# An expert's gate and up matmuls woven together, two in a row over the same tokens

## The chip, the cores and the metric

The kernel runs on one core of a Trainium2 chip. The metric is the device time of one execution in microseconds; before the change the median of three runs is 642.3 us (642.14 to 643.11).

## What is computed

4096 tokens of width 256 go through a cross-attention block and then through a mixture of 16 routed experts and one shared one. Everything is float32.

```
x = x + xattn(layernorm(x), ctx, ctx, mask)          # keys: 154 per batch
xf = layernorm(x)
logits = l2norm(xf) @ l2norm(gate_w).T               # 16 experts
scores = sigmoid(logits); top 8, weights normed to sum 1 -> combine
g = einsum('nd,edh->neh', xf, w_gate)                # D = 256, H = 128
u = einsum('nd,edh->neh', xf, w_up)
y = einsum('neh,ehd->ned', silu(g) * u, w_down)
out = x + einsum('ned,ne->nd', y, combine) + shared expert (same form, weight 1)
```

## The kernel before, in words

The tokens are cut into 8 chunks of 512. For each chunk the kernel runs 17 experts (expert 0 is the shared one), and beside the experts of chunk c it runs the attention, the second layernorm and the router of chunk c+1, in pieces that tables at the top of the file place at steps of the expert loop ("5.5" is behind the gate and up of step 5). No scheduler is at work: every engine has its own program, written out by hand, and executes it in order; semaphores join them.

Numbers stay float32 on the way, but the matmuls of the experts are made in three passes. Each operand is split into a high part (rounded to the fast float32 format of TensorE) and a low part (the rest), and `three_pass` (lines 394 to 400) issues high x high, high x low and low x high: lines 397, 398 and 399. So gate and up are each 2 (halves of D) x 3 = 6 matmuls of 512 columns, with weights as the stationary and tokens as the moving operand; `down` (L622) is 4 (tiles of tokens) x 3 = 12 matmuls of 256 columns. Gate, up and y have two PSUM banks each; expert e uses bank e mod 2 of gate and of up.

The chain of one expert e through the engines:

- PE: gate, 6 matmuls, then up, 6 matmuls (`gate`, `up`, both by `first_of`)
- ACT: `tanh_gate` (L880), reads the gate's bank
- DVE: `silu_up`: L1158 (silu, reads the gate's bank again) and L1162 (product with up's bank)
- POOL: `weighted` (L1358), times the tokens' routing weights
- ACT: `hidden_hi` (L887), and DVE: `hidden_lo` (L1168), the split of the result
- PE: `down`, 12 matmuls

What sets the order is the same loop on each engine, over steps s:

- PE: down(s), pieces of the front at s, gate(s+3) and up(s+3), pieces at s+.5
- ACT: tanh_gate(s+2), pieces at s, hidden_hi(s+1), in the first chunk the high part of a weight (L809), pieces at s+.5
- DVE: silu_up(s+2), pieces at s, hidden_lo(s+1), in the first chunk the low part of a weight (L1017), pieces at s+.5
- POOL: weighted(s+1), then its pieces

Waits that matter here: gate(e) waits until silu of e-2 has read its bank (`silu_done`), up(e) until the product of e-2 has read its bank (`prod_done`); down(e) waits for `h_hi` and `h_lo` of e, the two halves of the split.

Pieces of the front that are named below. On PE: `attend` at 5.5 and 6, which waits for the low part of the probabilities (`write_probs_lo`, DVE L1094 and L1096, themselves behind ACT L842 and L844 `write_probs_hi`); `logits` at 12 (L582, L584), which waits for the low part of the tokens (`write_t2_lo`, DVE L1068 twice, behind a DMA that brings the turned tokens back); `turn_z` (L589) and `turn_c` (L593), two small transposes of the router. On DVE: `swap_x2` (L1056) at 8.5, which starts that DMA's way, `ln2_scale` (L1032), `top_eight` and `weights` of the router. On POOL: `ln2_std` and `inverse_norm` (L1309 to L1341) and `add_bias` (L1320).

In the prologue of the first chunk the router's `turn_z(0)` stands between gate(0, 0) and up(0, 0):

```python
            gate(0, 0)
            turn_z(0)
            up(0, 0)
```

Of the kernel before, what the change touches and what calls it, by code (L numbers as in the profile page):

```python
# [17 lines left out]
HI, LO = 0, 1  # L18
# [17 lines left out]
def xattn_moe_kernel(nc, x, ctx, mask, Wq, bq, Wk, bk, Wv, bv, gate_w, w_gate, w_up, w_down,  # L36
                     sw_gate, sw_up, sw_down, out):
    B, S, D = x.shape
    KEYS = ctx.shape[1]
    E, _, H = w_gate.shape  # L40
    TOK = 512
    TILES = TOK // P
    HALF = TOK // 2
    CHUNKS = B * S // TOK
    KD = D // P
    NE = E + 1
# [7 lines left out]
    UP0, DN0 = KD * H, 2 * KD * H  # L54
    SCALE = float(D) ** -0.5
    REST = (B - 1) * KEYS
    AHEAD = 3
# [12 lines left out]
    with ExitStack() as stack:  # L70
        def sb(name, shape, dt=F32):
            return stack.enter_context(nc.sbuf_tensor(name, shape, dt))
# [5 lines left out]
        W = sb("W", [P, NE, 2, WCOLS], F32R)  # L78
# [4 lines left out]
        xT = sb("xT", [P, 2, 2, KD, TOK], F32R)  # L83
# [71 lines left out]
        def banks(name):  # L155
            return stack.enter_context(nc.psum_tensor(name, [P, 2, 512], F32))

        gate_ps, up_ps, y_ps, f_ps = (banks(n) for n in ("gate_ps", "up_ps", "y_ps", "f_ps"))
# [34 lines left out]
        FREE = 2  # L193
# [5 lines left out]
        def upto(c, per, k):  # L199

            return c * per + k
# [5 lines left out]
        def slot(c, e):  # L207

            return (NE * c + e) % 2

        def nxt(c, e):

            return (c, e) if e < NE else (c + 1, e - NE)

        def low_split(e):

            if e in POOL_SPLITS:
                return w_lo_pool, POOL_SPLITS.index(e) + 1
            return w_lo_dve, len([i for i in range(e + 1) if i not in POOL_SPLITS])
# [170 lines left out]
        def _(pe):  # L390
            mm = nc.tensor.matmul
            turn = nc.tensor.transpose

            def three_pass(ps, pairs, first, last):

                for i, ((lh, ll), (rh, rl)) in enumerate(pairs):
                    mm(ps, lh, rh, start=first and i == 0, stop=False)  # L397
                    mm(ps, lh, rl, start=False, stop=False)  # L398
                    ins = mm(ps, ll, rh, start=False, stop=last and i == len(pairs) - 1)  # L399
                return ins  # L400
# [186 lines left out]
            def turn_z(c):  # L587
                pe.wait_ge(z_read, upto(c, 1, 1))
                turn(f_ps[:, 0, 0:TILES * 2 * E], zT[:, 0:P], ident[:]).then_inc(z_turned, 1)  # L589

            def turn_c(c):
                pe.wait_ge(combined, upto(c, 1, 1))
                turn(f_ps[0:TILES * E, 1, 0:P], cw.rearrange("p j e -> p (j e)"), ident[:]).then_inc(c_turned, 1)  # L593

            def first_of(c, e, ps, col, free, done):
                i, par = slot(c, e), c % 2
                if e == 0:
                    pe.wait_ge(t2_hi, upto(c, 2, 2))
                    pe.wait_ge(t2_lo, upto(c, 2, 2))
                if c == 0:  # L600
                    pe.wait_ge(w_hi, e + 1)
                    pe.wait_ge(*low_split(e))
                    if e == 0:
                        pe.wait_ge(gate_split, 2)
                    if e == 1:
                        pe.wait_ge(a_read, 2)
                pe.wait_ge(free, upto(c, NE, e - 1 + FREE))
                ins = three_pass(ps[:, i, :], [((W[:, e, HI, col + k * H:col + (k + 1) * H],
                                                 W[:, e, LO, col + k * H:col + (k + 1) * H]),
                                                (xT[:, par, HI, k, :], xT[:, par, LO, k, :])) for k in range(KD)],  # L610
                                 first=True, last=True)
                ins.then_inc(done, 1)

            def gate(c, e):
                c, e = nxt(c, e)
                first_of(c, e, gate_ps, 0, silu_done, gate_done)

            def up(c, e):
                c, e = nxt(c, e)
                first_of(c, e, up_ps, UP0, prod_done, up_done)  # L620

            def down(c, e):  # L622
                i = slot(c, e)
# [57 lines left out]
            turn_ln2_first(1)  # L681
            keys_by_wq_rest(1)
            logits(0)
            gate(0, 0)
            turn_z(0)
            up(0, 0)
            gate(0, 1)
            up(0, 1)
            turn_c(0)
            values(2, f_ps[:, 0, 0:D])  # L690
            gate(0, 2)
            up(0, 2)
            values(3, f_ps[:, 1, 0:D])
            for c in range(CHUNKS):
                ahead = c + 1 < CHUNKS
                for s in range(NE):
                    if not ahead and s + AHEAD == NE - 1:

                        gate(c, NE - 1)
                        up(c, NE - 1)  # L700
                    down(c, s)
                    if ahead:
                        front(s, c + 1)
                    if (s + AHEAD < NE - 1 or ahead) and not (c == 0 and s == 1):
                        gate(c, s + AHEAD)
                        up(c, s + AHEAD)
                    if c == 0 and s == 0:

                        gate(c, s + AHEAD + 1)
                        up(c, s + AHEAD + 1)  # L710
                    if ahead:
                        front(s + .5, c + 1)

# [714 lines left out]
```

## Time and profile before

| what | value |
|---|---|
| median of 3 runs | 642.3 us |
| the profiled execution: its time | 641.74 us |
| its span, first to last instruction | 639.6 us |
| PE busy | 632.1 us (99%), 3690 matmuls |
| PE weight loads | 550.9 us (86%) |
| DVE busy | 464.7 us (73%) |
| POOL busy | 275.4 us (43%) |
| ACT busy | 234.6 us (37%) |
| DMA, share of 16 engines | 36% |
| granted clock of TensorE, mean | 0.999 |
| chain that ended last: PE's share | 92% |

A busy time is the union of an engine's instructions, and a matmul's record reaches to its modelled end, past the start of the next one: what a matmul costs in a dense stream is the distance from its start to the next start, not its length. What lies between the span and the execution's own time (2.1 us) is taken as fixed. A name such as "gate_ps<-xT,W" says what an instruction writes and what it reads.

### The profile page before, as it was taken

How to read it: one execution, taken by the hardware profiler on the slowest of the kernel's cores; microseconds unless marked ns; L12 is line 12 of the kernel's file. 1: busy time of each engine (PE TensorE's matmuls, PEld its weight loads, DVE VectorE, ACT ScalarE, POOL GpSimd, SP SyncE). 2: the span in 40 equal slices, each digit the busy share in tenths (PEclk: the TensorE clock that was granted, in tenths of full speed). 3: DMA queues.
4: the chain of work that ended last, by engine and by line, in shares of the span. 5: the costliest groups of instructions: out<-in, count | busy, mean ns of one | idle time of the engine just before them, and what ended most of it. 6: DMA issues, size and time to landing. Idle time of an engine off the chain costs nothing.

```text
span 639.6 us, 10415 instructions
## 1 busy us (share of the span) xinstructions
PE 632.1 (99%) x3690; PEld 550.9 (86%) x3690; DVE 464.7 (73%) x925; ACT 234.6 (37%) x500; POOL 275.4 (43%) x261
## 2 busy tenths in 40 slices
PE   8999999999999999999999999999999999999997
PEld 7688888988889888888888888888888888888886
DVE  3789887759876698767977689766987669575444
ACT  4745544332343324333242333324233332432221
POOL 2527576325533356233653346423562335423342
PEclk9999999999999999999999999999999999999999
DMA  7457562532315324333335232253151431242100
GB/s 206 100 178 218 162 169 44 201 101 73 83 35 182 109 67 99 111 107 119 68 68 188 70 117 66 34 200 108 67 98 38 162 109 46 53 133 101 66 2 33
DMA packets 112512, 67.04 MB, mean 105 GB/s; under 512 B 80981, under 2 KB 102254, under 8 KB 112462
## 3 DMA queue, kind: packets, MB, share of 16 engines
q1 hardware_dynamic: 111374, 65.61, 35.4%
q10 hardware_dynamic: 1088, 0.79, 0.4%
q8 instruction: 29, 0.48, 0.3%
q14 instruction: 21, 0.17, 0.1%
HBM read 55.66 MB, written 10.42 MB: 103 GB/s over the span
## 4 chain that ended last, share of the span: by engine, by line
PE 92%; DVE 3%; DMA 1%; issue 1%; ACT 1%; POOL 1%; SPq 1%; POOLq 0%; ACTq 0%; DVEq 0%
PE gate_ps L399 9%; PE gate_ps L398 9%; PE y_ps L397 9%; PE up_ps L399 9%; PE up_ps L398 9%; PE gate_ps L397 9%; PE y_ps L398 9%; PE up_ps L397 9%; PE y_ps L399 9%; PE f_ps L545 3%; PE up_ps L406 1%; PE f_ps L582 1%; SPq L277 1%; PE f_ps L584 1%; DMA xs<-t_rows 1%
## 5 line engine op out<-in xcount | busy, mean ns | idle before, releaser
L1358 POOL TENSOR_TENSOR hidden<-hidden,cb 128x512 f32<-128x512 f32 x128 | 193.3, 1511 | 288.6 <-DVE hidden L1162 245.6
L880 ACT ACTIVATE hidden<-gate_ps 128x512 f32<-128x512 f32 x136 | 81.3, 598 | 295.0 <-PE gate_ps L399 294.9
L1158 DVE SCALAR_TENSOR_TENSOR hidden<-hidden,gate_ps 128x512 f32<-128x512 f32 x136 | 92.7, 682 | 97.5 <-ACT hidden L880 97.2
L397 PE MATMUL y_ps<-W,hs 128*128 128x256 f32 x544 | 154.2, 283 | 0.6 <-DVE hs L1168 0.6
L398 PE MATMUL y_ps<-W,hs 128*128 128x256 f32 x544 | 151.5, 278 | 0.0
L399 PE MATMUL y_ps<-W,hs 128*128 128x256 f32 x544 | 151.2, 278 | 0.0
L1168 DVE TENSOR_TENSOR hs<-hidden,hs 128x512 fp32r<-128x512 f32 x136 | 105.6, 777 | 22.6 <-ACT hs L887 22.2
L397 PEld LDWEIGHTS y_ps<-W,hs 128*128 128x128 f32 x544 | 102.2, 188 | 7.4 <-issue 1.6
L397 PE MATMUL gate_ps<-xT,W 128*128 128x512 f32 x272 | 107.3, 394 | 0.0
L399 PE MATMUL gate_ps<-xT,W 128*128 128x512 f32 x272 | 107.1, 394 | 0.0
L399 PE MATMUL up_ps<-xT,W 128*128 128x512 f32 x272 | 106.9, 393 | 0.0
L398 PE MATMUL gate_ps<-xT,W 128*128 128x512 f32 x272 | 106.8, 393 | 0.0
L398 PE MATMUL up_ps<-xT,W 128*128 128x512 f32 x272 | 106.7, 392 | 0.0
L398 PEld LDWEIGHTS y_ps<-W,hs 128*128 128x128 f32 x544 | 102.7, 189 | 4.3
L397 PE MATMUL up_ps<-xT,W 128*128 128x512 f32 x272 | 106.1, 390 | 0.0
L1162 DVE TENSOR_TENSOR hidden<-hidden,up_ps 128x512 f32<-128x512 f32 x136 | 93.5, 687 | 13.5 <-PE up_ps L399 0.5
L399 PEld LDWEIGHTS y_ps<-W,hs 128*128 128x128 f32 x544 | 102.5, 188 | 0.0
L887 ACT ACTIVATE hs<-hidden 128x512 fp32r<-128x512 f32 x136 | 85.2, 626 | 39.6 <-POOL hidden L1358 30.6
L398 PEld LDWEIGHTS up_ps<-xT,W 128*128 128x128 f32 x272 | 51.1, 188 | 11.6
L397 PEld LDWEIGHTS up_ps<-xT,W 128*128 128x128 f32 x272 | 51.1, 188 | 11.5
L399 PEld LDWEIGHTS gate_ps<-xT,W 128*128 128x128 f32 x272 | 51.1, 188 | 10.7
L399 PEld LDWEIGHTS up_ps<-xT,W 128*128 128x128 f32 x272 | 51.1, 188 | 10.6
(164 smaller groups left out, 641.1 us busy)
## 6 DMA issues: line engine op xcount, KB each, us to landing
cb<-c_rows SPq DMA_DIRECT2D x64, 512.0 KB, 4.5
blocks<-in_x_dram SPq DMA_DIRECT2D x28, 128.0 KB, 2.9
xin<-in_x_dram SPq DMA_DIRECT2D x7, 512.0 KB, 3.7
t_rows<-blocks SPq DMA_DIRECT2D x28, 128.0 KB, 2.7
xs<-t_rows SPq DMA_DIRECT2D x7, 512.0 KB, 3.6
out_dram<-x SPq DMA_DIRECT2D x7, 512.0 KB, 5.8
p_rows<-blocks SPq DMA_DIRECT2D x28, 80.0 KB, 2.3
stage<-in_L_ffn_w_gate_dram SPq DMA_DIRECT2D x16, 128.0 KB, 2.7
```

What stands on the lines that cost most here:

```text
L277: sp.dma_start(to[q].rearrange("b r k j a -> b (r k j) a"), t_blocks[q * SQ:(q + 1) * SQ].rearrange("b r k j a -> b (r k j) a")) \
L397: mm(ps, lh, rh, start=first and i == 0, stop=False)
L398: mm(ps, lh, rl, start=False, stop=False)
L399: ins = mm(ps, ll, rh, start=False, stop=last and i == len(pairs) - 1)
L406: turn(up_ps[:, 0, 0:P], ident[:], ident[:])
L545: ins = mm(to, xs[:, k, j * P:(j + 1) * P], A[:, c // 2, k, :], start=k == 0, stop=k == KD - 1)
L880: af(ew[:, i, :], gate_ps[:, i, :], ACT.Tanh, scale=0.5).then_inc(tanh_done, 1)
L887: af(hs[:, i, HI, :], h[:, i, :], ACT.Copy).then_inc(h_hi, 1)
L1158: V_.scalar_tensor_tensor(out=ew[:, i, :], in0=ew[:, i, :], scalar=1.0, in1=gate_ps[:, i, :], op0=ALU.add, op1=ALU.mult).then_inc(silu_don ...
L1162: V_.tensor_tensor(ew[:, i, :], ew[:, i, :], up_ps[:, i, :], ALU.mult).then_inc(prod_done, 1)
L1168: V_.tensor_tensor(hs[:, i, LO, :], h[:, i, :], hs[:, i, HI, :].bitcast(F32), ALU.subtract) \
L1358: pg.tensor_tensor(h[:, i, :], ew[:, i, :], cb[:, pair % PLACES, (e - 1) % 2, :], ALU.mult) \
```

## The change

`first_of`, `gate` and `up` go, and `gate_up` takes their place. It waits for both banks at once, and then issues the twelve matmuls in pairs: for each half of D and each of the three passes first the gate's matmul and then up's, with the same moving tokens. Gate's last matmul, the eleventh of the twelve, signals `gate_done`; up's last, the twelfth, `up_done`.

```diff
-            def first_of(c, e, ps, col, free, done):
+            def gate_up(c, e):
+
+                c, e = nxt(c, e)
                 i, par = slot(c, e), c % 2
...
-                pe.wait_ge(free, upto(c, NE, e - 1 + FREE))
-                ins = three_pass(ps[:, i, :], [((W[:, e, HI, col + k * H:col + (k + 1) * H],
-                                                 W[:, e, LO, col + k * H:col + (k + 1) * H]),
-                                                (xT[:, par, HI, k, :], xT[:, par, LO, k, :])) for k in range(KD)],
-                                 first=True, last=True)
-                ins.then_inc(done, 1)
...
+                pe.wait_ge(silu_done, upto(c, NE, e - 1 + FREE))
+                pe.wait_ge(prod_done, upto(c, NE, e - 1 + FREE))
+                for k in range(KD):
+                    for n, (w, m) in enumerate(((HI, HI), (HI, LO), (LO, HI))):
+                        start, stop = k == 0 and n == 0, k == KD - 1 and n == 2
+                        moving = xT[:, par, m, k, :]
+                        g = mm(gate_ps[:, i, :], W[:, e, w, k * H:(k + 1) * H], moving, start=start, stop=stop)
+                        u = mm(up_ps[:, i, :], W[:, e, w, UP0 + k * H:UP0 + (k + 1) * H], moving, start=start, stop=stop)
+                g.then_inc(gate_done, 1)
+                u.then_inc(up_done, 1)
...
-            gate(0, 0)
+            gate_up(0, 0)
             turn_z(0)
-            up(0, 0)
-            gate(0, 1)
-            up(0, 1)
+            gate_up(0, 1)
             turn_c(0)
...
                     down(c, s)
                     if ahead:
                         front(s, c + 1)
                     if (s + AHEAD < NE - 1 or ahead) and not (c == 0 and s == 1):
-                        gate(c, s + AHEAD)
-                        up(c, s + AHEAD)
+                        gate_up(c, s + AHEAD)
```

The number of matmuls, their sizes and operands, and all other engines' programs stay. PE at the start of the expert phase, first expert of the first chunk (f_ps by L589 is `turn_z`), before:

```order
L397 MATMUL gate_ps<-xT,W 128x512 [waits w_lo_pool,gate_split,w_hi,silu_done,t2_lo,t2_hi]
L398 MATMUL gate_ps<-xT,W 128x512
L399 MATMUL gate_ps<-xT,W 128x512
L397 MATMUL gate_ps<-xT,W 128x512
L398 MATMUL gate_ps<-xT,W 128x512
L399 MATMUL gate_ps<-xT,W 128x512
L589 MATMUL f_ps<-ident,zT 128x128 [waits z_read]
L397 MATMUL up_ps<-xT,W 128x512 [waits w_lo_pool,gate_split,w_hi,prod_done,t2_lo,t2_hi]
```

and with the change:

```order
L616 MATMUL up_ps<-xT,W 128x512
L615 MATMUL gate_ps<-xT,W 128x512
L616 MATMUL up_ps<-xT,W 128x512
L615 MATMUL gate_ps<-xT,W 128x512
L616 MATMUL up_ps<-xT,W 128x512
L589 MATMUL f_ps<-ident,zT 128x128 [waits z_read]
L615 MATMUL gate_ps<-xT,W 128x512 [waits silu_done,a_read,prod_done,w_lo_pool,w_hi]
```

The router's transpose has moved behind all twelve matmuls of the first expert. The second place is any later expert, PE between two `down`s (y_ps), before:

```order
L397 MATMUL gate_ps<-xT,W 128x512 [waits silu_done,w_lo_pool,w_hi]
L398 MATMUL gate_ps<-xT,W 128x512
L399 MATMUL gate_ps<-xT,W 128x512
L397 MATMUL gate_ps<-xT,W 128x512
L398 MATMUL gate_ps<-xT,W 128x512
L399 MATMUL gate_ps<-xT,W 128x512
L397 MATMUL up_ps<-xT,W 128x512 [waits prod_done,w_lo_pool,w_hi]
L398 MATMUL up_ps<-xT,W 128x512
L399 MATMUL up_ps<-xT,W 128x512
L397 MATMUL up_ps<-xT,W 128x512
L398 MATMUL up_ps<-xT,W 128x512
L399 MATMUL up_ps<-xT,W 128x512
```

and with the change:

```order
L615 MATMUL gate_ps<-xT,W 128x512 [waits silu_done,prod_done,w_lo_pool,w_hi]
L616 MATMUL up_ps<-xT,W 128x512
L615 MATMUL gate_ps<-xT,W 128x512
L616 MATMUL up_ps<-xT,W 128x512
L615 MATMUL gate_ps<-xT,W 128x512
L616 MATMUL up_ps<-xT,W 128x512
L615 MATMUL gate_ps<-xT,W 128x512
L616 MATMUL up_ps<-xT,W 128x512
L615 MATMUL gate_ps<-xT,W 128x512
L616 MATMUL up_ps<-xT,W 128x512
L615 MATMUL gate_ps<-xT,W 128x512
L616 MATMUL up_ps<-xT,W 128x512
```

The gate's last matmul has moved from sixth to eleventh place, up's stays twelfth, and the wait for `prod_done` has moved from the seventh matmul to the first.

## Rows read from the trace of the kernel before

**Rows 1.** Busy time by stretch, six chunks: us, PE, PEld, DVE, ACT, POOL, clock, DMA share, GB/s

```profile
108.70:562.60 453.90, 453.83 (x2679) 399.35 (x2679) 342.07 (x674) 156.39 (x336) 191.31 (x175) 1.00 0.34 98
```

**Rows 2.** Timeline of PE, experts 7 and 8 of a chunk: start us, length us

```profile
215.82 0.39 PE L397 MATMUL gate_ps<-xT,W 128*128 128x512 f32 x1
...
217.19 0.39 PE L397 MATMUL up_ps<-xT,W 128*128 128x512 f32 x1
...
218.56 0.28 PE L397 MATMUL y_ps<-W,hs 128*128 128x256 f32 x1
...
222.70 0.28 PE L397 MATMUL f_ps<-V,xT 128*128 128x256 f32 x1
```

**Rows 3.** Timeline of PE, expert 4 of that chunk

```profile
203.37 0.40 PE L397 MATMUL gate_ps<-xT,W 128*128 128x512 f32 x1
203.60 0.40 PE L398 MATMUL gate_ps<-xT,W 128*128 128x512 f32 x1
203.84 0.40 PE L399 MATMUL gate_ps<-xT,W 128*128 128x512 f32 x1
204.07 0.40 PE L397 MATMUL gate_ps<-xT,W 128*128 128x512 f32 x1
```

**Rows 4.** Timeline of ACT, same chunk, tanh of expert 7

```profile
217.39 0.60 ACT L880 ACTIVATE hidden<-gate_ps 128x512 f32<-128x512 f32 x1 [3.02 <-PE gate_ps L399]
```

**Rows 5.** Timeline of DVE, same chunk, around steps 5, 8 and 13

```profile
218.02 0.69 DVE L1158 SCALAR_TENSOR_TENSOR hidden<-hidden,gate_ps 128x512 f32<-128x512 f32 x1 [2.04 <-ACT hidden L880]
218.83 0.69 DVE L1162 TENSOR_TENSOR hidden<-hidden,up_ps 128x512 f32<-128x512 f32 x1
219.71 1.73 DVE L1094 TENSOR_TENSOR xT<-xn,xT 128x512 fp32r<-128x512 f32 x1 [0.19 <-ACT ptail L844]
221.47 0.68 DVE L1096 TENSOR_TENSOR ptail<-xn,ptail 32x512 fp32r<-32x512 f32 x1
...
234.98 1.71 DVE L1032 TENSOR_SCALAR xn<-x,meanvar,small 128x256 f32<-128x256 f32 x2
...
240.01 0.68 DVE L1168 TENSOR_TENSOR hs<-hidden,hs 128x512 fp32r<-128x512 f32 x1
...
257.10 0.69 DVE L1168 TENSOR_TENSOR hs<-hidden,hs 128x512 fp32r<-128x512 f32 x1 [1.49 <-ACT hs L887]
```

**Rows 6.** Timeline of POOL, same chunk

```profile
219.60 1.29 POOL L1358 TENSOR_TENSOR hidden<-hidden,cb 128x512 f32<-128x512 f32 x1 [2.45 <-DVE hidden L1162]
...
229.77 1.29 POOL L1358 TENSOR_TENSOR hidden<-hidden,cb 128x512 f32<-128x512 f32 x1 [0.70 <-DVE hidden L1162]
...
234.42 1.80 POOL L1358 TENSOR_TENSOR hidden<-hidden,cb 128x512 f32<-128x512 f32 x1
...
247.96 1.85 POOL L1320 TENSOR_TENSOR keepb<-keep,brow 128x616 f32<-128x616 f32 x1
```

**Rows 7.** Timeline of PE, same chunk: down(10), logits, down(14)

```profile
241.12 0.28 PE L397 MATMUL y_ps<-W,hs 128*128 128x256 f32 x1
...
250.78 0.63 PE L582 MATMUL f_ps<-xT,G 128*32 128x512 f32 x2
...
258.75 0.28 PE L397 MATMUL y_ps<-W,hs 128*128 128x256 f32 x1
```

**Rows 8.** Timeline of DVE, first chunk: product of expert 0, hidden_lo of expert 10

```profile
38.66 0.69 DVE L1162 TENSOR_TENSOR hidden<-hidden,up_ps 128x512 f32<-128x512 f32 x1
...
87.75 0.68 DVE L1168 TENSOR_TENSOR hs<-hidden,hs 128x512 fp32r<-128x512 f32 x1
```

**Rows 9.** Timeline of PE, first chunk: turn_z, gate of expert 2, down(10)

```profile
33.98 0.30 PE L589 MATMUL f_ps<-ident,zT 128*128 128x128 f32 x1
...
39.26 0.58 PE L397 MATMUL gate_ps<-xT,W 128*128 128x512 f32 x1
...
88.58 0.36 PE L397 MATMUL y_ps<-W,hs 128*128 128x256 f32 x1
```

**Rows 10.** Line 1068 in the window 240 to 256: ns min/median/max, starts

```profile
L1068 DVE TENSOR_TENSOR xT<-xs,xT x2: 790/1340/1891, 247.8 to 248.5; 128x512 fp32r<-128x512 f32 x2
```

**Rows 11.** Timeline of POOL, last chunk, weighting of the last expert

```profile
631.24 1.29 POOL L1358 TENSOR_TENSOR hidden<-hidden,cb 128x512 f32<-128x512 f32 x1 [1.07 <-DVE hidden L1162]
```

**Rows 12.** Timeline of ACT, last chunk, high part of the last expert

```profile
633.21 0.63 ACT L887 ACTIVATE hs<-hidden 128x512 fp32r<-128x512 f32 x1 [0.73 <-PE y_ps L399]
```

More of the change, by code:

```diff
@@ L606, in first_of @@
                         pe.wait_ge(a_read, 2)
-                pe.wait_ge(free, upto(c, NE, e - 1 + FREE))
-                ins = three_pass(ps[:, i, :], [((W[:, e, HI, col + k * H:col + (k + 1) * H],
-                                                 W[:, e, LO, col + k * H:col + (k + 1) * H]),
-                                                (xT[:, par, HI, k, :], xT[:, par, LO, k, :])) for k in range(KD)],
-                                 first=True, last=True)
-                ins.then_inc(done, 1)
[L614 to L620, printed above, removed]
+                pe.wait_ge(silu_done, upto(c, NE, e - 1 + FREE))
[8 more added lines that the diff above has]
+                u.then_inc(up_done, 1)
             def down(c, e):
@@ L683, in _ @@
             logits(0)
-            gate(0, 0)
+            gate_up(0, 0)
             turn_z(0)
-            up(0, 0)
-            gate(0, 1)
-            up(0, 1)
+            gate_up(0, 1)
             turn_c(0)
             values(2, f_ps[:, 0, 0:D])
-            gate(0, 2)
-            up(0, 2)
+            gate_up(0, 2)
             values(3, f_ps[:, 1, 0:D])
@@ L697, in _ @@
                     if not ahead and s + AHEAD == NE - 1:
-                        gate(c, NE - 1)
-                        up(c, NE - 1)
+                        gate_up(c, NE - 1)
                     down(c, s)
@@ L704, in _ @@
                     if (s + AHEAD < NE - 1 or ahead) and not (c == 0 and s == 1):
-                        gate(c, s + AHEAD)
-                        up(c, s + AHEAD)
+                        gate_up(c, s + AHEAD)
                     if c == 0 and s == 0:
-                        gate(c, s + AHEAD + 1)
-                        up(c, s + AHEAD + 1)
+                        gate_up(c, s + AHEAD + 1)
                     if ahead:
```

## The prediction, made before the changed kernel had run

> **What bounds the kernel.** I read the busy times by stretch first. From 108.70 to 562.60 us, six whole chunks, PE is busy 453.83 of 453.90 us at a granted clock of 1.00, the upper level of 2.4 GHz [rows 1]: in this stretch PE never waits, each chunk takes 453.9 / 6 = 75.65 us, and every microsecond by which PE is made to wait is a microsecond of the result. Then PE's timeline. Gate's six matmuls take from 215.82 to 217.19, up's six from 217.19 to 218.56 [rows 2]: 1.37 / 6 = 0.228 us for a matmul of 512 columns, the same inside a bank as over the change of bank at 217.19. Two things can therefore move the time: the 0.228 us, and the slack that the other engines have against PE. So I read next, on ACT, DVE and POOL, what every `down`, `attend` and `logits` waits for, and how long before it that was ready.
>
> **Term 1, the rate of the matmuls: 0.** 8 x 17 x 12 = 1632 matmuls are reordered, none is removed, and each keeps its weight load. Their distance does not follow what they share. In gate's block now the first two matmuls have the same weights and other tokens, the third has other weights and other tokens, and up's first another bank, and gate's and up's six take the same 1.37 us [rows 2]. Some blocks run at (204.07 - 203.37) / 3 = 0.233 us [rows 3], again at every kind of step alike. From that, pairs over the same tokens into alternating banks should run at 0.228 too. Both ends stay open: 0.233 upwards, and downwards 512 columns at 2.4 GHz, 0.213. I take 0.228, as that is what nearly all blocks show over every kind of step.
>
> **Term 2, the gate arrives later.** Gate's last matmul moves from sixth to eleventh place, by 5 x 0.228 = 1.14 us; up's last stays. ACT stands idle 3.02 us before tanh of expert 7, waiting for just that [rows 4], so tanh starts at 217.39 + 1.14 = 218.53. Silu follows it by 0.63 us [rows 4, 5]: 219.16 to 219.85, and the product starts at 219.88 in place of 218.83: 1.05 us later. Formerly tanh and silu ran while PE made up; that cover is gone. All that is behind the product (POOL's weighting, both halves of the split) comes 1.05 to 1.14 us later against PE. Nothing of this costs anything where `down` had more slack than that, and mostly it had. Where it had not, PE waits. In a repeating chunk these are the places, in order:
>
> *attend at 5.5.* DVE L1094 waits for ACT's L844, which stands behind tanh of expert 7. It started at 219.71 and took 1.73 us, ending 0.55 us after POOL's weighting (219.60 to 220.89) [rows 5, 6]. Now POOL starts at 220.65, L1094 at 220.85: POOL is still first, ends at 221.94, L1094 at 222.49, L1096 at 223.20 in place of 222.15. The attend started at 222.70 [rows 2], so it can't before 223.25: **0.55 us**. If DVE came first here, it would be 0.
>
> *down(10).* The high price is on a queue. POOL's weighting of expert 9 (229.77) follows its product, and behind it stand the small steps of the second layernorm and then the weighting of expert 10 (234.42 to 236.22), with no idle time before it [rows 6]; L1032 on DVE (234.98, 1.71 us) ends 0.47 us after it, and from there DVE runs without a break to the low part of expert 10, 240.01 to 240.69, for down(10) at 241.12 [rows 5, 7]. All of it moves by 1.05. Slack is 0.43, less the handover from DVE to PE, which in the first chunk, where down(10) did wait, is 88.58 - (87.75 + 0.68) = 0.15 [rows 8, 9]. So 1.05 - 0.28 = **0.77 us**; at least 0, if L1032 slips ahead of POOL.
>
> *logits at 12.* Of the two L1068 the first took 0.79 and the second 1.89 us [rows 10]: the second ended at 250.36, 0.55 us after POOL's L1320 (247.96 + 1.85 = 249.81) [rows 6], and logits started at 250.78 [rows 7]. L1320 stands behind the weighting of expert 13 and moves by 1.05, to 250.86; L1068 then ends at 251.41, and logits start at 251.56: **0.78 us**. Here it matters whether L1068 waits for the whole of L1320 or only runs slower beside it: 0.79 beside 1.89 us, and an end 0.55 us behind POOL's in two places, say that it waits. The Trainium skill ("SBUF — State Buffer", section "Who interferes with whom") says that VectorE and GpSimd share one pair of ports as an exclusive lock, and that the later one blocks fully. By that rule the term is the one above; if the two shared the bandwidth instead, it would be near 0 and the whole sum 4.7 us less. By that rule, the trace agrees.
>
> *down(14), down(15).* The low part of expert 14 ends at 257.79, down(14) started at 258.75 [rows 5, 7]: slack 0.96 - 0.15 = 0.81, against 1.05: **0.24**. For down(15) the same reckoning gives another 0.09 (its rows are not shown).
>
> The other `down`s of a chunk, read one by one, all had more left than the shift and cost nothing. The new wait of the gate for `prod_done` of e-2 costs nothing either: product 7 would be done at about 220.6, and gate 9 comes behind the attend of 222.70. Together 0.55 + 0.77 + 0.78 + 0.33 = 2.43 us for a chunk, and six such chunks: **14.6 us**. They add up, as a gate that PE issues behind a stall carries the stall to all that follows from it; where `down` comes behind the same stall as well, as down(15) behind down(14), I have taken it off.
>
> **Term 3, the first chunk.** `turn_z` starts at 33.98 [rows 9]; now six more matmuls are ahead of it, 1.37 us. On it hang router, silu and product of expert 0; the latter ends at 38.66 + 0.69 = 39.35 [rows 8] and would end at 40.72. The gate of expert 2 started at 39.26 and halted 0.2 us for silu 0 [rows 9]; now it needs product 0 first, so it starts at 40.8: 1.35 us. Then down(10), which has no slack at all there [rows 8, 9], costs the whole 1.05, and down(14), down(15), with some 0.2 less slack each than later, about 0.6. **3.0 us**.
>
> **Term 4, the end.** POOL's weighting of the last expert ended at 632.53 [rows 11], now 633.58; ACT's high part behind it started at 633.21, when PE freed its buffer [rows 12], now at 633.6: **0.4 us** for the last down, the last addition and the store behind it.
>
> Sum: 14.6 + 3.0 + 0.4 = 18.0 us. The profiled execution took 641.7 us; it becomes 659.7. The median of the runs is 0.6 us above that execution, so the forecast is **660.3 us**. A measurement of this kernel can tell from no change about 0.2%, 1.3 us.
>
> **Rivals.**
>
> *A, as worked out*, 660.3: chance 0.70.
>
> *B, slower, but the meetings of DVE and POOL fall out better.* DVE gets ahead of POOL at L1094, L1032 or L1068; in the first case by as little as 0.2 us. At the lowest, all three at 0, a chunk costs 0.33, and the sum is 2.0 + 3.0 + 0.4 = 5.4: 647.7 us; with one or two of them 652 to 656. Against it: POOL and DVE move by the same amount, so their order stays. 0.12.
>
> *C, slower still: the blocks settle at 0.233 us* [rows 3]. 1632 x 0.005 = 8.2 us more: 668.5. That pace exists, but is rare. 0.05.
>
> *D, faster: the pairs run quicker.* If 0.228 holds something that the order of operands or the return to the same PSUM bank causes, pairs over the same tokens could come down to 0.213: 1632 x 0.015 = 24.5 us less, 659.7 - 24.5 + 0.6 = 635.8 us. It decides from 18.0 / 1632 = 0.011 us, that is below 0.217. Against it: bank changes and repeats of weights, which exist already, gain nothing [rows 2]; and the slack of every `down` would shrink by the same hundredths times twelve or more, which eats part of it. The Trainium skill ("TensorE: Matmul & The Clock Gate", section "Back-to-back issue gap") gives about 216 ns for 512 columns, so by that page some 12 ns a matmul are there to be had; the trace disagrees with that figure, at 228. 0.08.
>
> *E, no change*, 642.3: the 1.1 us vanish in slack everywhere. Against it stand PE's 99.98% in the six chunks and the first chunk's down(10) without slack. 0.05.
>
> **The numbers.** D is faster: 0.08. E is the same: 0.05. A, B, C are slower: 0.87. The range reaches from B's lowest case to the edge of C, 648 to 668, and leaves out D, E and half of C.
>
> **What would show it.** Gate and up alternating at 0.228 us (right) or elsewhere (C, D). ACT's idle time before tanh as long as before, but the product behind silu at once, with no wait for up. PE with about 2.4 us of waits in each of the chunks between: a gap before the first f_ps<-V,xT, before the y_ps of expert 10 and before L582; PE busy some 97% of such a stretch; chunks of 78.1 us instead of 75.65. The expert phase starting 1.35 us late from expert 2 on. Wrong it is if chunks stay at 75.65 us, or if the 0.228 us moves.

## The result, and the profile after the change

The changed kernel takes 661.63 us (median of 5 runs, 661.35 to 661.96); the kernel before, run between them on the same chip, 642.14 us. The ratio is 1.031 (95% interval 1.0298 to 1.0320): 3.1% slower, 19.5 us. The profiled execution took 661.63 us too, its span is 659.5 us in place of 639.6. Of all the executions reported below one ran at a granted clock of 0.687 and took 861.69 us (the kernel with the merged wait alone); it is left out of that kernel's figures.

From the page of the changed kernel, the busy times and the group of tanh (busy, mean ns | idle before). Line numbers from gate and up on are 8 smaller than before: tanh is L872, silu L1150, the product L1154, `hidden_lo` L1160, `weighted` L1350.

```profile
PE 638.8 (97%) x3690; PEld 548.0 (83%) x3690; DVE 470.7 (71%) x925; ACT 233.8 (35%) x500; POOL 279.7 (42%) x261
...
L872 ACT ACTIVATE hidden<-gate_ps 128x512 f32<-128x512 f32 x136 | 81.3, 598 | 335.9 <-PE gate_ps L615 335.9
```

The same group before:

```profile
L880 ACT ACTIVATE hidden<-gate_ps 128x512 f32<-128x512 f32 x136 | 81.3, 598 | 295.0 <-PE gate_ps L399 294.9
```

Tanh has not become longer (598 ns), nor has the product (687 ns in both pages); ACT has 41 us more idle time before tanh, all of it waiting for the gate. Next the busy time of the six whole chunks, the answer to [rows 1] (us, PE, PEld, DVE, ACT, POOL, clock, DMA share, GB/s):

```profile
111.53:581.53 470.00, 460.23 (x2678) 397.22 (x2677) 347.17 (x672) 155.43 (x336) 194.27 (x175) 1.00 0.33 95
```

Six chunks take 470.00 us in place of 453.90, 78.33 each, and PE is idle for 9.8 of them, where before it was idle for 0.07. (The time grew by 16.1, the idle time by 9.7. A PE that resumes after a wait shows busy at once and only then finds its pace, and a record's modelled end covers part of each gap: distances between starts, not busy times, give what a wait costs.) The views by wait and by time say where it halts. Three of PE's waits over the whole execution (us, times, longest; three more waits of the attend, 1.4 us, stand in that view under "issue"), then the timeline of one chunk, the answer to [rows 2, 7]:

```profile
PE y_ps L397 <- DVE hs L1160: 4.5, 9, 0.6
PE f_ps L582 <- DVE xT L1060: 3.1, 5, 0.7
PE f_ps L397 <- DVE ptail L1088: 1.5, 3, 0.5
```

```profile
225.55 0.39 PE L615 MATMUL gate_ps<-xT,W 128*128 128x512 f32 x1
...
228.07 0.40 PE L616 MATMUL up_ps<-xT,W 128*128 128x512 f32 x1
228.96 0.36 PE L397 MATMUL f_ps<-V,xT 128*128 128x256 f32 x1 [0.49 <-DVE ptail L1088]
229.15 0.28 PE L398 MATMUL f_ps<-V,xT 128*128 128x256 f32 x1
...
247.34 0.40 PE L616 MATMUL up_ps<-xT,W 128*128 128x512 f32 x1
248.22 0.36 PE L397 MATMUL y_ps<-W,hs 128*128 128x256 f32 x1 [0.48 <-DVE hs L1160]
248.42 0.28 PE L398 MATMUL y_ps<-W,hs 128*128 128x256 f32 x1
...
257.83 0.28 PE L399 MATMUL y_ps<-W,hs 128*128 128x256 f32 x1
258.69 0.62 PE L582 MATMUL f_ps<-xT,G 128*32 128x512 f32 x2 [0.59 <-DVE xT L1060]
...
266.44 0.39 PE L616 MATMUL up_ps<-xT,W 128*128 128x512 f32 x1
266.91 0.36 PE L397 MATMUL y_ps<-W,hs 128*128 128x256 f32 x1
```

Three facts stand here. The twelve woven matmuls run at (228.07 - 225.55) / 11 = 0.229 us, the pace of before. The first matmul behind the block comes 0.89 us (attend), 0.88 (`down(10)`), 0.86 (logits, behind a `down`) and 0.47 (`down(14)`) after its forerunner, in place of 0.23 or 0.11. And behind a matmul of 256 columns that had to wait, the second comes only after 0.19 or 0.20 us, where any other two are 0.11 or 0.12 apart: 0.08 us more for the halt. That holds at attend, `down(10)` and `down(14)` (266.91, then 267.11). It does not at logits, 512 columns with 32 columns of weights: its first two matmuls take 0.46 us after the wait (258.69 to 259.15) and 0.47 where there was none (571.82 to 572.29).

Only five of the six chunks halt at logits. In the last of them POOL has no `add_bias` to do, and logits follow the last matmul of `down` (571.71) by 0.11 us, with no wait:

```profile
571.82 0.63 PE L582 MATMUL f_ps<-xT,G 128*32 128x512 f32 x2
```

ACT and DVE of the chunk of the timeline, the answer to [rows 4, 5]:

```profile
224.13 0.60 ACT L872 ACTIVATE hidden<-gate_ps 128x512 f32<-128x512 f32 x1 [3.02 <-PE gate_ps L615]
```

```profile
224.77 0.69 DVE L1150 SCALAR_TENSOR_TENSOR hidden<-hidden,gate_ps 128x512 f32<-128x512 f32 x1 [2.12 <-ACT hidden L872]
225.49 0.69 DVE L1154 TENSOR_TENSOR hidden<-hidden,up_ps 128x512 f32<-128x512 f32 x1
226.45 1.65 DVE L1086 TENSOR_TENSOR xT<-xn,xT 128x512 fp32r<-128x512 f32 x1 [0.27 <-ACT ptail L836]
228.13 0.68 DVE L1088 TENSOR_TENSOR ptail<-xn,ptail 32x512 fp32r<-32x512 f32 x1
...
242.37 1.71 DVE L1024 TENSOR_SCALAR xn<-x,meanvar,small 128x256 f32<-128x256 f32 x2
...
247.40 0.68 DVE L1160 TENSOR_TENSOR hs<-hidden,hs 128x512 fp32r<-128x512 f32 x1
...
255.22 3.33 DVE L1060 TENSOR_TENSOR xT<-xs,xT 128x512 fp32r<-128x512 f32 x2 [0.18 <-ACT xT L816]
...
266.07 0.69 DVE L1160 TENSOR_TENSOR hs<-hidden,hs 128x512 fp32r<-128x512 f32 x1 [1.49 <-ACT hs L879]
```

The product now follows silu by 0.03 us. Before, it followed by 0.12 [rows 5] and started 0.11 us behind the end of up's last matmul, which is why it comes 1.05 us later and not 1.14. That matmul, before:

```profile
218.33 0.39 PE L399 MATMUL up_ps<-xT,W 128*128 128x512 f32 x1
```

Each of PE's halts ends 0.14 to 0.15 us after a DVE end: 228.81 to 228.96, 248.08 to 248.22, 258.55 to 258.69, 266.76 to 266.91. POOL (the answer to [rows 6]) is still first at each of the three meetings with DVE that the forecast priced, before attend, before `down(10)` and before logits:

```profile
226.25 1.29 POOL L1350 TENSOR_TENSOR hidden<-hidden,cb 128x512 f32<-128x512 f32 x1 [2.46 <-DVE hidden L1154]
...
241.82 1.79 POOL L1350 TENSOR_TENSOR hidden<-hidden,cb 128x512 f32<-128x512 f32 x1
...
254.51 1.68 POOL L1350 TENSOR_TENSOR hidden<-hidden,cb 128x512 f32<-128x512 f32 x1 [1.00 <-DVE hidden L1154]
256.15 1.84 POOL L1312 TENSOR_TENSOR keepb<-keep,brow 128x616 f32<-128x616 f32 x1
```

### The profile page after: what moved, and what is told of

It is laid out like the page before. It is cut to its first block, busy times and chain, and to the rows that moved or that the text cites. A ratio compares the mean times of both kernels' runs of the same rounds, so it can differ in the third digit from the quotient of the medians.

```text
span 659.5 us, 10522 instructions
## 1 busy us (share of the span) xinstructions
PE 638.8 (97%) x3690; PEld 548.0 (83%) x3690; DVE 470.7 (71%) x925; ACT 233.8 (35%) x500; POOL 279.7 (42%) x261
## 4 chain that ended last, share of the span: by engine, by line
PE 72%; DVE 12%; DMA 6%; ACT 3%; issue 3%; SPq 2%; POOL 1%; POOLq 0%; ACTq 0%; DVEq 0%
PE gate_ps L615 21%; PE up_ps L616 21%; PE y_ps L397 7%; PE y_ps L398 7%; PE y_ps L399 7%; DMA xs<-t_rows 3%; PE f_ps L545 3%; DVE xn L1024 2%; DVE xT L1060 2%; DMA t_rows<-blocks 2%; DVE hs L1160 1%; SPq L277 1%; DVE hidden L1154 1%; DVE hidden L1150 1%; DVE blocks L1048 1%
## 5 line engine op out<-in xcount | busy, mean ns | idle before, releaser
L1350 POOL TENSOR_TENSOR hidden<-hidden,cb 128x512 f32<-128x512 f32 x128 | 194.1, 1518 | 300.0 <-DVE hidden L1154 267.4
L872 ACT ACTIVATE hidden<-gate_ps 128x512 f32<-128x512 f32 x136 | 81.3, 598 | 335.9 <-PE gate_ps L615 335.9
L1150 DVE SCALAR_TENSOR_TENSOR hidden<-hidden,gate_ps 128x512 f32<-128x512 f32 x136 | 93.1, 685 | 137.1 <-ACT hidden L872 136.7
L615 PEld LDWEIGHTS gate_ps<-xT,W 128*128 128x128 f32 x816 | 153.4, 188 | 30.2 <-issue 0.6
L1160 DVE TENSOR_TENSOR hs<-hidden,hs 128x512 fp32r<-128x512 f32 x136 | 105.4, 775 | 16.1 <-ACT hs L879 15.2
L1154 DVE TENSOR_TENSOR hidden<-hidden,up_ps 128x512 f32<-128x512 f32 x136 | 93.5, 687 | 4.6
L1301 POOL TENSOR_SCALAR small<-meanvar 128x2 f32<-128x2 f32 x32 | 11.4, 355 | 32.4 <-DVE meanvar L1018 31.0
L1303 POOL TENSOR_TENSOR small<-small,minus_half 128x2 f32<-128x2 f32 x32 | 23.1, 723 | 2.7
L1295 POOL TENSOR_TENSOR W<-stage,W 128x768 fp32r<-128x768 f32 x8 | 15.4, 1936 | 18.3 <-ACT W L801 18.3
L1060 DVE TENSOR_TENSOR xT<-xs,xT 128x512 fp32r<-128x512 f32 x14 | 19.0, 1393 | 2.5 <-ACT xT L816 2.4
L545 PE MATMUL f_ps<-A,xs 128*128 128x154 f32 x128 | 19.3, 294 | 0.0
L545 PEld LDWEIGHTS f_ps<-A,xs 128*128 128x128 f32 x128 | 18.0, 190 | 0.7 <-issue 0.2
```

The lines of the kernel that those rows point to most:

```text
L545: ins = mm(to, xs[:, k, j * P:(j + 1) * P], A[:, c // 2, k, :], start=k == 0, stop=k == KD - 1)
L615: g = mm(gate_ps[:, i, :], W[:, e, w, k * H:(k + 1) * H], moving, start=start, stop=stop)
L872: af(ew[:, i, :], gate_ps[:, i, :], ACT.Tanh, scale=0.5).then_inc(tanh_done, 1)
L1150: V_.scalar_tensor_tensor(out=ew[:, i, :], in0=ew[:, i, :], scalar=1.0, in1=gate_ps[:, i, :], op0=ALU.add, op1=ALU.mult).then_inc(silu_don ...
L1154: V_.tensor_tensor(ew[:, i, :], ew[:, i, :], up_ps[:, i, :], ALU.mult).then_inc(prod_done, 1)
L1160: V_.tensor_tensor(hs[:, i, LO, :], h[:, i, :], hs[:, i, HI, :].bitcast(F32), ALU.subtract) \
```

## The experiments

Two theories stand against each other. **The place theory**, mine: only the place at which the gate's last matmul stands among the twelve counts, and the price is paid at the few spots where PE had little slack. **The rival**: the weaving itself (alternating banks, the same moving tokens twice, the merged wait) costs or gives something.

### The merged wait alone

The kernel before, with the wait for the product added at the gate:

```diff
                 pe.wait_ge(free, upto(c, NE, e - 1 + FREE))
+                if free is silu_done:
+                    pe.wait_ge(prod_done, upto(c, NE, e - 1 + FREE))
```

> The kernel before with the gate also waiting for prod_done of e-2; no weaving. Theory (the late gate signal makes the time): that wait has over 2 us left everywhere in a repeating chunk, so 642.1 us as before, at most 0.5 more from the start. Rival (holding both banks before the first matmul is what costs): a good part of the 19.5 us, over 650.

Measured: 641.61 us (9 runs), ratio 0.9996 (0.9986 to 1.0007). The wait is free.

### The place of the gate's last matmul, woven and not

The changed kernel, whose loop takes its order from a string, one letter for each of the twelve matmuls; everything else stays, and `turn_z` stands behind the first expert's twelve, as in the change.

```diff
-                for k in range(KD):
-                    for n, (w, m) in enumerate(((HI, HI), (HI, LO), (LO, HI))):
...
+                for which in "gggggguuuuuu":
+                    ps, col, done = banks_of[which]
+                    n = made[which]
+                    k, w, m = passes[n]
+                    ins = mm(ps[:, i, :], W[:, e, w, col + k * H:col + (k + 1) * H], xT[:, par, m, k, :],
+                             start=n == 0, stop=n == 5)
+                    made[which] += 1
+                    if n == 5:
+                        ins.then_inc(done, 1)
```

Sixth place, the string above:

> The changed function with its merged waits and the router's transpose behind the first expert, but gate's six matmuls ahead of up's six: gate ends in sixth place. Theory: only the start is left of the change, 642.1 + 1.4 = 643.5 us. Rival (something in the repeating chunks other than gate's place costs): clearly over 645.

Seventh place, `"ggggguguuuuu"`:

> Order g g g g g u g u u u u u, gate ends in seventh place. Theory: the product comes 0.14 us later, less than the slack of about 0.4, 0.4 and 0.25 that attend, down(10) and logits have left by the measured waits, so as with place six, 643.5 us. Rival (cost in proportion to the delay): a fifth of 18 us more, 647.

Ninth place, `"ggguguguguuu"`:

> Order g g g u g u g u g u u u, gate ends in ninth place; product 0.59 us later. Theory: waits of about 0.19 at attend, 0.19 at down(10), 0.34 at logits, none at down(14), and 0.08 for each restart, 0.95 us for a chunk, 5.7 in six, 1.4 at the start, 0.6 in the first chunk: 650 us. Rival (in proportion, three fifths of 18 us, and the start): 654. A rival by which weaving costs from the first pair on: 655 and more.

Twelfth place, woven, up ahead of gate in each pair, `"ugugugugugug"`:

> Woven as the change, but up ahead of gate in each pair, so gate ends in twelfth place. Theory: only the place of gate's last matmul counts, so the same as up first unwoven, 667.5 us, within 1 us of it. Rival (weaving as such costs): clearly slower than up first unwoven.

Twelfth place, not woven, `"uuuuuugggggg"`:

> No weaving at all: up's six matmuls, then gate's six, so gate ends in twelfth place instead of eleventh; otherwise as the change. Theory: tanh comes 6 x 0.228 = 1.37 us later than before the change and the product 1.28; the four waits of a chunk grow by 0.23 each, 6 x 0.9 = 5.5 us, and some 0.5 in the first and last chunk: 667.5 us. Rival (the alternation of banks and weights slows PE): without alternation most of the 19.5 us go, under 650.

| order | gate's last | us (runs) | ratio to before, 95% | six chunks, us | a chunk, over sixth place |
|---|---|---|---|---|---|
| gggggguuuuuu | 6 | 643.07 (10) | 1.0014 (1.0004 to 1.0024) | 453.97 | 0 |
| ggggguguuuuu | 7 | 643.70 (10) | 1.0015 (1.0001 to 1.0029) | 454.40 | 0.07 |
| ggguguguguuu | 9 | 649.28 (4) | 1.0102 (1.0085 to 1.0118) | 459.32 | 0.89 |
| the change | 11 | 661.63 (5) | 1.0309 (1.0298 to 1.0320) | 470.00 | 2.67 |
| ugugugugugug | 12 | 670.92 (4) | 1.0446 (1.0429 to 1.0464) | 477.66 | 3.95 |
| uuuuuugggggg | 12 | 670.46 (4) | 1.0443 (1.0427 to 1.0458) | 477.91 | 3.99 |

In these kernels the line numbers from gate and up on are 4 larger than in the changed kernel (`hidden_lo` is L1164, `write_t2_lo` L1064). The row of the six chunks at sixth place, at ninth place, and at twelfth place not woven and woven, one fence for each kernel:

```profile
109.86:563.83 453.97, 453.88 (x2679) 399.36 (x2678) 343.65 (x675) 156.35 (x336) 190.22 (x175) 1.00 0.34 98
```

```profile
110.37:569.69 459.32, 457.49 (x2679) 398.68 (x2678) 345.98 (x672) 156.06 (x336) 191.14 (x175) 1.00 0.33 97
```

```profile
113.45:591.36 477.91, 463.63 (x2678) 396.96 (x2677) 347.41 (x671) 155.35 (x336) 194.14 (x175) 1.00 0.33 93
```

```profile
112.61:590.27 477.66, 463.43 (x2678) 396.82 (x2677) 348.79 (x671) 155.48 (x336) 194.58 (x175) 1.00 0.32 93
```

The place theory holds and its rival falls: what weaving itself costs or gives is too small to show here. Twelve matmuls in two unbroken blocks and twelve in strict alternation, with the gate last in both, differ by 0.46 us, inside both intervals. With the gate at sixth place PE is idle for 0.09 us in six chunks, although the loop, the merged wait and the place of `turn_z` are the change's. The price is also not linear in the shift: 0.07 us a chunk for one place, 0.89 for three, 2.67 for five. That is a threshold, as slack gives it. With the slacks of the prediction (0.50 at the attend, 0.28 at `down(10)`, 0.27 at logits, 0.81 at `down(14)`) and 0.08 for a halt at attend and `down(10)`, a shift of three places (the product 3 x 0.228 - 0.09 = 0.59 later) gives 0.09 + 0.31 + 0.32 + 2 x 0.08 = 0.88 against 0.89, and one place (0.14 later) gives 0. The single terms fit less well than the sum: in two chunks whose starts I compared, attend halted for 0.16 and 0.20 us and not for 0.09.

At the twelfth place I had expected 3 us too little. The waits of PE there, the unwoven kernel:

```profile
PE y_ps L397 <- DVE hs L1164: 8.9, 19, 0.9
```

Nineteen recorded waits of a `down` in place of nine. Six of the ten more are at `down(14)`, which also halted in the changed kernel, too briefly to be recorded; the others lie in the first chunk and at the end. The distances between starts show two new halts in each of the chunks compared, both too short for that view: `down(3)` (0.19 to 0.26 us) and `down(8)` (0.18 to 0.19 us) had more slack than the change's shift of 1.05, but not more than 1.28. A sum over today's waits holds only until the next slack runs out.

### The router's transpose back between gate and up of the first expert

The change, with the very first expert in the old order, `turn_z(0)` between its gate and its up:

```diff
-            def gate_up(c, e):
+            def gate_up(c, e, between=None):
...
-            gate_up(0, 0)
-            turn_z(0)
+            gate_up(0, 0, lambda: turn_z(0))
```

> The change, but the very first expert keeps the old order, gate, the router's transpose, up. Theory: the router of the first chunk is 1.37 us earlier, which all behind it passes on: 661.6 - 1.35 = 660.3 us. Rival (the start is hidden behind later waits of the first chunk): 661.6, no change.

Measured: 661.30 us (4 runs), ratio 1.0298 (1.0282 to 1.0314), beside 1.0309 (1.0298 to 1.0320) of the change. By the times alone the difference, 0.7 us by the ratios, is unclear: the intervals overlap. The sixth-place kernel shows the same edit from the other side: its chunks are those of before, `turn_z` stands behind all twelve, and it is 0.9 us slower than before (0.3 to 1.5). The traces show the mechanism. In the changed kernel:

```profile
39.39 0.30 PE L593 MATMUL f_ps<-ident,route 128*64 128x128 f32 x1 [1.05 <-DVE route L1143]
...
40.79 0.47 PE L615 MATMUL gate_ps<-xT,W 128*128 128x512 f32 x1 [0.23 <-DVE hidden L1154]
...
53.41 0.39 PE L397 MATMUL y_ps<-W,hs 128*128 128x256 f32 x1
...
91.51 0.36 PE L397 MATMUL y_ps<-W,hs 128*128 128x256 f32 x1 [0.65 <-DVE hs L1160]
```

The router's second transpose waits 1.05 us for what hangs on the first, and gate(2) for the product of expert 0. At 53.41 us the changed kernel is 1.42 us behind the kernel before (51.99 us); with the first expert apart that `down` starts at 51.92 us, and the second chunk at 110.22 us, 1.31 sooner than in the change. Of the 53.41 - 51.92 = 1.49 us and of the 1.31, 0.13 had come up before the experts, so the traces give 1.2 to 1.4 us; the times, at 0.7 or less, neither confirm nor refute that. I take 0.7 to 1.4 us for this part.

### Taking the waits away one by one: logits

POOL's `add_bias` (L1312, L1320 before) placed one step later, so that it doesn't meet `write_t2_lo` (L1060, L1068 before):

```diff
-POOL_SOON = dict(add_bias=(12.5,), ln1_std=(11.5, 11.5))
+POOL_SOON = dict(add_bias=(13.5,), ln1_std=(11.5, 11.5))
```

> The change, with POOL's add_bias moved from step 12.5 to 13.5, away from the second L1060 (L1068 before) that the logits wait for. Theory (VectorE waits for the whole of add_bias): the wait of 0.75 us at logits and its restart go in each of six or seven chunks: 661.6 - 5 = 656.6 us. Rival (logits wait for the DMA of the turned tokens or for silu's late start): 661.6, no change.

Measured: 658.29 us (4 runs), ratio 1.0244 (1.0229 to 1.0259), 3.3 us less than the change by the medians. The line of `write_t2_lo` in one chunk (ns least/median/most) and the logits of the next:

```profile
L1060 DVE TENSOR_TENSOR xT<-xs,xT x2: 677/1152/1628, 254.3 to 255.9; 128x512 fp32r<-128x512 f32 x2
```

```profile
334.99 0.63 PE L582 MATMUL f_ps<-xT,G 128*32 128x512 f32 x2
```

And the six chunks:

```profile
111.40:577.91 466.51, 460.04 (x2679) 397.79 (x2677) 341.95 (x672) 155.38 (x336) 192.39 (x175) 1.00 0.33 95
```

Logits follow the last matmul of `down` (here 334.88) by 0.11 or 0.12 us in five of the six chunks, and by 0.15 in the first of them. With `add_bias` out of the way DVE's second half takes 0.68 us in place of 1.88; the first (254.30 to 255.93) still takes 1.63, held up by the weighting, which ends at 255.39. So the cause of this wait is shown: DVE's second half, held up behind a second POOL operation. The six chunks gain 3.5 us, 0.70 for each of the five that had waited, where I had put 0.75 and a restart of 0.08 on each of six or seven.

### down(10), with and without the weaving

The same, and `inverse_norm` one step later, so that POOL reaches the weighting of expert 10 sooner:

```diff
-POOL_AT = dict(ln2_std=(7.5, 8.5), inverse_norm=(8.5,))
+POOL_AT = dict(ln2_std=(7.5, 8.5), inverse_norm=(9.5,))
...
-POOL_SOON = dict(add_bias=(12.5,), ln1_std=(11.5, 11.5))
+POOL_SOON = dict(add_bias=(13.5,), ln1_std=(11.5, 11.5))
```

> The change with add_bias at 13.5 as before and also POOL's inverse_norm (four small operations, 2.0 us) moved from step 8.5 to 9.5, behind the weighting of expert 10. Theory (down(10) waits by way of POOL's queue): the weighting starts 0.5 us earlier, right behind its product, ends at once and lets L1160 and L1024 of VectorE end some 0.35 us earlier; the wait at down(10) falls from 0.65 to 0.3 us, over six or seven chunks 2 to 2.5 us: 656 us. Rival (POOL has no part in it, VectorE's own queue is late): 658.3, as without this move.

Measured: 659.45 us (5 runs), ratio 1.0272 (1.0258 to 1.0286): 1.2 us more than with `add_bias` alone. A miss. PE comes to `down(10)` 0.37 to 0.45 us late in place of 0.63 to 0.67, but `down(9)` now comes 0.15 to 0.23 late, where it had not been late at all, and in one chunk logits 0.19. In the first chunk `down(10)` waits 1.6 us in place of some 0.65, and from its first expert to its end that chunk became 0.7 us longer. POOL's weighting of expert 10 does start 0.6 us sooner (241.22 in place of 241.82). It now holds up DVE's first L1024 in place of the second, with the low part of expert 9 (L1160, 242.69) behind it:

```profile
241.22 1.40 POOL L1350 TENSOR_TENSOR hidden<-hidden,cb 128x512 f32<-128x512 f32 x1 [1.45 <-DVE hidden L1154]
```

```profile
241.05 1.71 DVE L1024 TENSOR_SCALAR xn<-x,meanvar,small 128x256 f32<-128x256 f32 x2
242.69 0.68 DVE L1160 TENSOR_TENSOR hs<-hidden,hs 128x512 fp32r<-128x512 f32 x1
```

The collision was moved, not removed: from the product of expert 10 to the end of both L1024, DVE takes as long as before (to the transpose behind them 3.60 us in this kernel and in the changed one). That the forecast's chain holds `down(10)` up is borne out by the halts that moved with it; no kernel here is without the halt. The same two edits on the kernel before:

> The kernel before with both moves of POOL's pieces (add_bias to 13.5, inverse_norm to 9.5). Theory: in the repeating chunks PE never waits, so nothing is to be had there; at most some tenths in the first chunk: 642.0 us, no difference that can be measured. Rival (these meetings of POOL and VectorE cost the kernel before too): 640 or less.

Measured: 642.89 us (11 runs), ratio 1.0005 (0.9996 to 1.0014): no difference. Where PE has slack everywhere, these places of POOL's work are worth nothing.

### attend, with the high part of the probabilities sooner

My step for the attend says that `write_probs_hi` on ACT stands behind a tanh that now comes late. So it goes ahead of that tanh, beside the later `add_bias`:

```diff
-ACT_AT = dict(exps=(1.5, 2), probs_hi=(5,), t2_hi=(11.5,), read_z=(12.5,), tanh_scores=(13,), combine_rows=(15,))
+ACT_AT = dict(exps=(1.5, 2), probs_hi=(4.5,), t2_hi=(11.5,), read_z=(12.5,), tanh_scores=(13,), combine_rows=(15,))
...
-POOL_SOON = dict(add_bias=(12.5,), ln1_std=(11.5, 11.5))
+POOL_SOON = dict(add_bias=(13.5,), ln1_std=(11.5, 11.5))
```

> The change with add_bias at 13.5 (as in the run that had it alone, 658.3 us) and ScalarE's write_probs_hi at step 4.5 in place of 5, ahead of the tanh of expert 7 and no longer behind it. Theory (attend waits because its probabilities stand behind the late tanh): L1086 of VectorE then starts right behind the product of expert 7 and ahead of POOL, the wait of 0.65 us at attend and its restart of 0.08 go in each of seven chunks: 658.3 - 5 = 653.3 us. Rival (attend waits for the probabilities' DMA, or POOL wins the port all the same): 658.3, no change.

Measured: 661.38 us (4 runs), ratio 1.0295 (1.0261 to 1.0329): 3.1 us above the kernel with `add_bias` alone. A miss for both expectations. Two things happen: the operation now stands on ACT in front of a tanh and waits for its DMA (seven times, 8.2 us in all), and in the first chunk the low part of the probabilities meets POOL's work. One of these ACT operations, then the attend of the first chunk on PE, then DVE and POOL there:

```profile
226.81 0.63 ACT L834 ACTIVATE xT<-xn 128x512 fp32r<-128x512 f32 x1 [1.84 <-DMA xn<-p_rows]
```

```profile
74.24 0.55 PE L397 MATMUL f_ps<-V,xT 128*128 128x256 f32 x1 [2.30 <-DVE ptail L1088]
```

```profile
70.06 2.37 DVE L1086 TENSOR_TENSOR xT<-xn,xT 128x512 fp32r<-128x512 f32 x1
72.46 1.63 DVE L1088 TENSOR_TENSOR ptail<-xn,ptail 32x512 fp32r<-32x512 f32 x1
```

```profile
70.03 1.85 POOL L1295 TENSOR_TENSOR W<-stage,W 128x768 fp32r<-128x768 f32 x1 [3.04 <-ACT W L801]
71.84 1.71 POOL L1350 TENSOR_TENSOR hidden<-hidden,cb 128x512 f32<-128x512 f32 x1
```

The second chunk then starts 4.5 us later (at 115.88 us, with `add_bias` alone at 111.40); 0.35 of that had come up before the experts. The halt itself is 2.5 us of it. Another 1.5 us come behind it: after these 2.3 us of idle time PE's granted clock is 0.51, the lower of its two levels, for 3.2 us, and the matmuls of 256 columns start 0.21 us apart in place of 0.12. The stretch (us, PE, PEld, DVE, ACT, POOL, clock, DMA share, GB/s):

```profile
74.24:77.45 3.21, 3.21 (x15) 3.21 (x16) 2.88 (x6) 0.70 (x1) 1.24 (x1) 0.51 0.59 196
```

Further on it helps: the last three of the six chunks take 232.31 us, 77.44 each, where the six with `add_bias` alone take 77.75 on average. The attend comes 0.61 to 0.67 us late with `add_bias` alone; here it is 0.27 to 0.32 in four of the six chunks and 0.88 and 0.56 in the two in which ACT waited longest for the DMA (1.84 and 1.46 us, against 1.03 to 1.21 in the four). So the late tanh holds about half of this wait; what holds the other 0.3, and whether a place without the DMA's wait would remove it, stays open.

None of the eleven kernels beats the kernel before.

## Why the prediction was right, step by step

The forecast was 660.3 us and the measurement is 661.63. Of its rivals, B (DVE ahead of POOL) falls with POOL being first at all three meetings, C (0.233 us) and D (pairs run quicker) with 0.229 us a matmul and with the unwoven twelfth place being as fast as the woven one, E with PE's waits.

| step of the prediction | predicted | measured |
|---|---|---|
| rate of the matmuls | 0 | 0 (0.229 us a matmul; woven against unwoven 0.46 us apart) |
| attend, a chunk | 0.55 | 0.62 to 0.67 |
| `down(10)`, a chunk | 0.77 | 0.65 to 0.74 |
| logits, a chunk | 0.78 | 0.67 to 0.75 in five of six, 0 in the sixth |
| `down(14)`, `down(15)`, a chunk | 0.33 | 0.33 to 0.39 |
| finding the pace again, 3 halts a chunk | not seen | 0.24 |
| steps of under 0.1 us, not put down to anything, a chunk | not seen | 0.2 |
| **six chunks** | **14.6** | **16.1** |
| first chunk | 3.0 | 2.8 |
| behind the six chunks | 0.4 | 0.95 |
| **sum** | **18.0** | **19.9** |

**Term 1 was right.** What two matmuls in a row share doesn't set their distance in this kernel. The prediction weighed a figure of some 216 ns for 512 columns from the Trainium skill ("TensorE: Matmul & The Clock Gate", section "Back-to-back issue gap") and let the trace decide. The Trainium skill gives it there as the gap of an isolated matmul, and some 131 ns for a sustained stream. The runs give 0.229 us in pairs over the same tokens, so neither figure is reached by this order.

**Term 2 was right in its mechanism and short by one item.** Of the mechanism all parts are seen: tanh with the same 3.02 us of idle time [rows 4], the product right behind silu, the halts exactly at attend, `down(10)`, logits, `down(14)`, each 0.15 us behind the DVE operation that was named. The prices hold to 0.1 us, but for logits: the forecast counted that wait six times, and the sixth chunk has no `add_bias`, so the trace itself shows the chunk without the meeting and without the wait. What was left out is that most halts cost more than their wait: 0.08 us until the second matmul, three times a chunk, 1.4 us in six chunks. It is the largest item that was missing; about another microsecond lies in steps of under 0.1 us that I can't name. So part of the closeness is luck: the wait counted once too often takes 0.8 us of the miss back, and the median of the runs, which lay on the profiled execution this time and not 0.6 us above it, another 0.6.

**The lock of DVE and POOL was right.** At logits, L1060 ends at 258.55, 0.56 us after POOL's L1312 (256.15 + 1.84 = 257.99), as before the change (0.55), and with `add_bias` elsewhere the wait is gone. That agrees with the blocking of the later engine as the Trainium skill has it ("SBUF — State Buffer", section "Who interferes with whom"); sharing the bandwidth would have made this term about 0.

**Term 3 was right in its size, not in its parts.** The start gave 1.42 us in place of 1.35 in the trace. Up to `down(10)` the delay grows to 91.51 - 88.58 = 2.93 us [rows 9] and not to 2.4: three `down`s of this chunk waited in place of one. Then logits, which had come 0.4 us late before (0.2 of it recorded as a wait), take that back, and `down(14)` and `down(15)` cost some 0.4 in place of 0.6.

**Term 4 was too small, since it followed the wrong expert.** I had taken the high part of the last expert, which now waits for POOL in place of PE, as predicted [rows 12], and starts 652.58 - 633.21 = 19.37 us later; 581.53 - 562.59 = 18.94 us of that had come up to the last chunk, so 0.43 us, as reckoned. But no PE wait hangs on it. What PE waits for last is the low part of the expert before it. ACT, POOL, DVE and PE of the changed kernel:

```profile
652.58 0.63 ACT L879 ACTIVATE hs<-hidden 128x512 fp32r<-128x512 f32 x1 [1.12 <-POOL hidden L1350]
```

```profile
651.27 1.28 POOL L1350 TENSOR_TENSOR hidden<-hidden,cb 128x512 f32<-128x512 f32 x1 [1.07 <-DVE hidden L1154]
```

```profile
651.49 1.60 DVE L1160 TENSOR_TENSOR hs<-hidden,hs 128x512 fp32r<-128x512 f32 x1 [0.30 <-ACT hs L879]
```

```profile
653.24 0.36 PE L397 MATMUL y_ps<-W,hs 128*128 128x256 f32 x1 [1.15 <-ACT hs L879]
```

The profile puts this wait down to ACT, whose high part of the last expert ends at 653.21. But 24 matmuls of `down` follow from here, two experts' worth, so this one is `down` of the expert before the last, and it needs that expert's low part.

Before, POOL's last weighting had been over at 632.53 [rows 11] when this low part started at 632.51: it took 0.69 us, and its `down` started at 633.35. Now the weighting starts 0.22 us ahead of it; the low part takes 1.60 and ends 0.54 us behind POOL. The `down` starts 0.15 us after the low part's end, 19.89 us later than before: 18.94, and 0.95 for this one new meeting.

## What to carry to other kernels

Before reordering matmuls, look for the engine that stands idle for a result of the block: the place of that result in the block is what the order sets, and sharing an operand was worth nothing here. A later result costs nothing up to the smallest slack and then its full excess at each spot in turn; read the slack of every consumer, and expect new spots beyond the ones that wait today. Count the halts as well as their lengths, and in an in-order program don't expect to buy a wait back by moving a neighbour: of three such moves one removed its wait, one moved the collision, and one put a wait for a DMA and a new collision in its place.

## What the runs showed of the hardware that was not expected

- A PE that had to wait loses 0.08 us beyond the wait: 0.19 to 0.20 us to the second matmul in place of 0.11 to 0.12 (256 columns), at attend, `down(10)` and `down(14)`. At logits (512 columns, 32 columns of weights) there is no such loss.
- After 2.30 us of idle time in the first chunk of the last experiment PE went on at a granted clock of 0.51 for 3.2 us, which cost it 1.5 us beside the halt of 2.5. After 1.61 us of idle time in the first chunk of the kernel with `inverse_norm` moved the clock stayed at 1.00.
- Six matmuls into one bank followed by six into the other, and twelve alternating between the banks, take the same time with the gate last in both: 670.46 and 670.92 us.
- The distance from POOL's end to the end of the TENSOR_TENSOR on DVE that it held up is nearly the same, whatever the lengths: 0.56 us for L1060 at logits and for L1086 at attend, 0.54 for L1160 at the end; the TENSOR_SCALAR L1024 before `down(10)` ends 0.47 us behind. In the first chunk of the last experiment L1086 (2.37 us, 0.69 in the change) and L1088 (1.63, 0.68 in the change) end 0.55 and 0.54 us behind two POOL operations in a row, so one edit on ACT let DVE meet two of them.
